# Fused attention and convolution, one core: the order of DVE, ACT and POOL work within a step rearranged

## The chip, the cores and the metric

The kernel runs on one core of a Trainium2 chip. TensorE (PE) multiplies matrices, VectorE (DVE) and ScalarE (ACT) read its results in PSUM, GpSimd (POOL) works on SBUF alone, and SyncE (SP) issues the transfers. The metric is device time in microseconds for one execution. Three runs of the kernel before took 2841.26, 2844.43 and 2851.31 us; the median, 2844.43, is the time to compare with.

## The reference

For each of four batches of 1024 rows by 1024 columns: a modulated RMS norm, attention with 16 heads of 64 and RMS-normalised queries and keys, an output product with a residual, and a causal depthwise convolution with four taps along the rows, whose taps come from `cond`.

```python
scale, shift = jnp.split(emb @ W_emb + b_emb, 2, axis=-1)
xn = _rms_norm(x, g_norm) * (1.0 + scale) + shift
q, k, v = ...                      # xn @ W_qkv, 16 heads of 64
q = _rms_norm(q, g_q)
k = _rms_norm(k, g_k)
attn = jax.nn.softmax(jnp.einsum('bhqd,bhkd->bhqk', q, k) * d ** (-0.5), axis=-1)
o = jnp.einsum('bhqk,bhkd->bhqd', attn, v)
x = x + (o + o @ W_out)            # o with the heads side by side
x = x + conv1d_causal(x, w=cond_2048) + b
```

## The kernel before

Every fp32 operand of a product is split into two fp16 halves, high and low, and a product is three matmuls. The high half is a rounded copy, the low half the difference, made on POOL.

`main` runs 32 **units** u, one for each batch and pair of heads. A unit has eight **steps** p0 to p7, one for each 128 query rows. In step p TensorE makes the scores of both heads (`score`, 12 matmuls of 512 columns); DVE takes each head's row maximum and forms the bias (`maximum`, L1216 and L1219, which also names the start of a step's DVE work); ACT makes the exponentials (`exponent`, L910), and the next step's scores wait for both, since they overwrite the same PSUM. The probabilities are rounded to the high half (`high`: ACT for head 0, L918, DVE for head 1, L1226), POOL makes the low halves (`low`, L1130), and SP transposes each (`transpose_p`). Two steps later `attend` multiplies them with the values in two parts: part 0 ends an odd step, part 1 follows the score of the next. Part 0 waits for the row of inverse sums, which ACT copies behind an odd step's exponentials (`inverse_rows`, L974).

Beside this runs, spread over the steps by hand, other work of other units:
- unit u+1's projections (`project`, p0 to p4) and queries and keys, in two halves: ACT `squares`, DVE `sums`, POOL `half_power` (the power -0.5, L1136), DVE `normalise` (two products, L1242 and L1246), ACT `high_halves` (L941), POOL `half_low` (L1141), TensorE `stacks` (transposes, L811), ACT `read_stacks`. The first score of the next unit needs the stacks that p7 makes;
- in batches 0 to 2, a row block of the next batch (`xs`): DVE `x_mean`, POOL `x_power`, DVE `x_multiply` and `x_shift`, ACT `x_high`, POOL `x_low`;
- from unit 8 on, the output product and convolution of the batch before (`outs`, `fins`): TensorE `out_product` in p5, p6, p7, ACT `read_y`, DVE `convolve` (L1299 to L1314), TensorE `out_transposes`, ACT `read_out`, SP `store_out`. `convolve` treats two chunks of 128 columns by turns: the copy of the halo, the first tap, the ends kept for the next rows, and three multiply-adds for each chunk.

The order on each engine is that of the code in its `unit`; an engine's queue is worked through in order, and semaphores join the engines. Nothing schedules it anew.

## Time and profile before

| | |
|---|---|
| median of three runs | 2844.43 us |
| the profiled execution: time, span | 2844.38 us, 2842.3 us |
| TensorE busy | 2447.5 us (86%) |
| DVE busy | 1947.2 us (69%) |
| POOL busy | 1727.9 us (61%) |
| ACT busy | 1582.1 us (56%) |
| mean granted clock of TensorE | 0.927 |
| main DMA queue, share of 16 engines | 80.1% |

The span runs from the first instruction to the last; the rest of the execution's time lies around it. "Busy" counts an engine's work, also where it is blocked inside an instruction. The first 203.8 us are `prepare` and the first projections, the last 140 the output products of the last batch.

### The profile page before, as it was taken

What the parts mean: (1) busy time and instruction counts of PE and PEld (TensorE: products, weight loads), DVE (VectorE), ACT (ScalarE), POOL (GpSimd) and SP (SyncE); (2) the same over time, 40 slices, a digit from 0 to 9 for tenths busy, and PEclk for the clock granted to TensorE, in tenths of its full rate; (3) what the DMA queues carried; (4) which work ended last, traced back from release to release, by engine and by line L of the source; (5) the groups of instructions that cost most, each with busy time, mean ns of one, the idle gap of its engine ahead of it and who ended that gap; (6) DMA issues with size and microseconds to landing.
All of it is one profiled execution on the core that took longest, in us unless ns stands there. A gap on an engine that the chain in (4) does not pass through costs nothing. (4 is left out here: it accounts for less than half of the span.)

```text
span 2842.3 us, 57564 instructions
## 1 busy us (share of the span) xinstructions
PE 2447.5 (86%) x20690; PEld 1570.7 (55%) x20690; DVE 1947.2 (69%) x2968; ACT 1582.1 (56%) x2575; POOL 1727.9 (61%) x972
## 2 busy tenths in 40 slices
PE   2468788887779999999899999999999998999688
PEld 0034445454446666565566565666566665666477
DVE  7655555555567777787787677778767777777644
ACT  2246565556556666566566666666555565665411
POOL 0057766666766777666667667666666666766510
PEclk8688898888899999999999999999999999999799
DMA  6858777778987897889988888889977878877751
GB/s 252 344 138 167 158 145 154 142 157 167 196 185 163 183 181 162 169 171 200 194 193 174 181 168 177 168 167 220 180 160 153 163 149 161 161 145 146 141 162 60
DMA packets 1234893, 487.28 MB, mean 171 GB/s; under 512 B 1139520, under 2 KB 1196992, under 8 KB 1232064
## 3 DMA queue, kind: packets, MB, share of 16 engines
q1 hardware_dynamic: 1234624, 483.63, 80.1%
q8 instruction: 177, 2.90, 0.4%
q14 instruction: 92, 0.75, 0.1%
HBM read 141.13 MB, written 57.18 MB: 70 GB/s over the span
## 5 line engine op out<-in xcount | busy, mean ns | idle before, releaser
L1130 POOL TENSOR_TENSOR p_pair<-prob,p_pair 128x1024 f16<-128x1024 f32 x512 | 1122.6, 2211 | 618.7 <-ACT p_pair L918 589.3
L799 PE MATMUL proj<-w_sb,xn_sb 128*128 128x384 f16 x6144 | 1029.1, 327 | 34.0 <-DMA xn_sb<-p_pair 29.3
L910 ACT ACTIVATE prob<-scores,bias,l_scale 128x1024 f32<-128x1024 f32 x512 | 616.1, 1203 | 765.7 <-DVE bias L1219 684.4
L1216 DVE TENSOR_REDUCE neg<-scores 128x1 f32<-128x1024 f32 x512 | 623.4, 1218 | 509.3 <-PE scores L748 497.8
L799 PEld LDWEIGHTS proj<-w_sb,xn_sb 128*128 128x128 f16 x6144 | 587.9, 98 | 435.2 <-DMA xn_sb<-p_pair 25.3
L748 PE MATMUL scores<-stack 64*128 64x512 f16 x3072 | 403.2, 398 | 52.7 <-ACT prob L910 34.4
L767 PE MATMUL values<-pT,v_pair 128*64 128x256 f16 x6144 | 431.8, 296 | 11.4 <-ACT inv_row L974 10.1
L767 PEld LDWEIGHTS values<-pT,v_pair 128*64 128x64 f16 x6144 | 345.0, 119 | 110.9 <-issue 82.0
L1226 DVE CAST p_pair<-prob 128x1024 f16<-128x1024 f32 x256 | 217.2, 848 | 157.5 <-ACT prob L910 153.7
L1314 DVE SCALAR_TENSOR_TENSOR acc<-yT,taps,acc 128x256 f32<-128x256 f32 x384 | 272.4, 775 | 5.5
L748 PEld LDWEIGHTS scores<-stack 64*128 64x128 f16 x3072 | 134.5, 98 | 250.2 <-issue 98.1
L823 PE MATMUL proj<-oT_in,wo 128*128 128x256 f16 x2304 | 267.9, 273 | 0.6
L918 ACT ACTIVATE p_pair<-prob 128x1024 f16<-128x1024 f32 x256 | 266.7, 1042 | 0.0
L1136 POOL TENSOR_TENSOR rs<-ms,power 128x16 f32<-128x16 f32 x64 | 202.2, 3159 | 62.7 <-DVE ms L1234 61.5
L823 PEld LDWEIGHTS proj<-oT_in,wo 128*128 128x128 f16 x2304 | 219.6, 98 | 33.7 <-issue 1.8
L811 PE MATMUL misc<-eye,qk_pair 128*128 128x128 f16 x512 | 51.7, 262 | 182.6 <-issue 106.7
L1141 POOL TENSOR_TENSOR qk_pair<-stage,qk_pair 128x512 f16<-128x512 f32 x128 | 157.4, 1252 | 6.5 <-ACT qk_pair L941 6.5
L811 PEld LDWEIGHTS misc<-eye,qk_pair 128*128 128x128 f16 x512 | 40.9, 117 | 190.0 <-issue 189.8
L926 ACT ACTIVATE stage<-proj 128x384 f32<-128x384 f32 x256 | 121.9, 476 | 39.6 <-PE proj L799 39.5
L1306 DVE TENSOR_SCALAR acc<-yT,taps,conv_b 128x256 f32<-128x256 f32 x128 | 128.3, 1043 | 0.0
L1219 DVE TENSOR_SCALAR bias<-neg,l_scale 128x1 f32<-128x1 f32 x512 | 109.7, 214 | 18.1
L1156 POOL TENSOR_TENSOR msx<-msx,power 128x1 f32<-128x1 f32 x32 | 18.0, 564 | 157.5 <-DVE msx L1251 142.9
(127 smaller groups left out, 2303.1 us busy)
## 6 DMA issues: line engine op xcount, KB each, us to landing
w_sb<-w_dram SPq DMA_DIRECT2D x128, 384.0 KB, 3.8
o_dram<-oT_pair SPq DMA_DIRECT2D x128, 128.0 KB, 2.6
out<-acc SPq DMA_DIRECT2D x64, 256.0 KB, 2.6
wq_raw<-in_L_cond_W_qkv SPq DMA_DIRECT2D x8, 1536.0 KB, 10.7
w_dram<-wq_pair SPq DMA_DIRECT2D x8, 1536.0 KB, 7.4
x_in<-in_x SPq DMA_DIRECT2D x24, 512.0 KB, 5.4
oT_in<-o_dram SPq DMA_DIRECT2D x12, 1024.0 KB, 5.9
xr<-in_x SPq DMA_DIRECT2D x24, 512.0 KB, 3.9
```

Of the source, the lines that this page charges most:

```text
L748: last = nc.tensor.matmul(scores[:, h, n * HN:(n + 1) * HN], stack[rows_, par, i, p * P:(p + 1) * P], stack[rows_, par, j, n * HN:(n + 1) ...
L767: last = nc.tensor.matmul(values[DH * h:DH * h + DH, 0:QG].rearrange("p (a n) -> p a n", a=2), v_pair[:, par, 2 * c + h, DH * i:DH * i + D ...
L799: last = nc.tensor.matmul(proj[:, t % 2, 0:6 * DH], xn_sb[:, t, i * K + c, :], w_sb[:, c, j, :], start=(c == 0 and i == j == 0), stop=(c = ...
L823: nc.tensor.matmul(dst, const["wo"][:, c, b, m * P:(m + 1) * P], oT_[:, c, a, :], start=(c == 0 and a == b == 0), stop=False)
L910: nc.scalar.activation(prob[:, h, :], scores[:, h, :], ACT.Exp, bias=bias[:, s:s + 1], scale=const["l_scale"][:, 0:1], accum_out=total[:, ...
L918: nc.scalar.activation(p_pair[:, s % 4, 0, :], prob[:, 0, :], ACT.Copy).then_inc(hi_a, 1)
L1130: nc.gpsimd.tensor_tensor(p_pair[:, s % 4, 1, :], prob[:, h, :], p_pair[:, s % 4, 0, :], ALU.subtract).then_inc(lo_done, 1)
L1136: nc.gpsimd.tensor_tensor(rs[:], ms[:], const["power"][:, 0:4 * KH], ALU.pow).then_inc(h_pw, 1)
L1141: last = nc.gpsimd.tensor_tensor(qk_pair[:, j, 1].rearrange("p t (h d) -> p (t h) d", d=DH), stage[:, hf, :, j * DH:(j + 1) * DH], qk_pair ...
L1216: nc.vector.tensor_reduce(neg[:, s:s + 1], scores[:, h, :], axis=AX.X, op=ALU.max, negate=True).then_inc(max_done, 1)
L1226: nc.vector.tensor_copy(p_pair[:, s % 4, 0, :], prob[:, 1, :]).then_inc(hi_b, 1)
L1314: nc.vector.scalar_tensor_tensor(out=acc[:, m, :], in0=yT[:, m, k:k + QG], scalar=const["taps"][:, k, c:c + 1], in1=acc[:, m, :], op0=ALU. ...
```

## The change

It moves work between places of a unit and splits one helper; no arithmetic is added or left out.
- `high`: DVE rounds head 0 and ACT head 1, in place of the other way round, and DVE does it right behind the maxima.
- `convolve` does one chunk; it is called four times a unit, in p7, p0 and p2 ahead of the maxima and behind `after_lows`, and in p3 behind `high`. Before, it was called in p7 and p1 with two chunks each, behind `high`. `out_transposes` and the store of the second half move from p2 and p4 to p4 and p6, and ACT's `read_out` with them.
- `x_multiply` and `x_shift` both stand in p1 ahead of the maxima, behind `after_lows`; `x_power` stands behind p0's low halves. The row block is loaded in p6 in place of p7.
- Second half of queries and keys: `half_power` stands between the two low halves of p5 (before: ahead of both), `normalise` and ACT's `high_halves` ahead of p6's maxima and exponentials (before: behind them), `half_low` ahead of p6's low halves (before: of p7's), `stacks` ahead of p7's output product (before: behind it).
- `sums` of the first half and `normalise` of the first half stand ahead of the maxima of p3 and p4.
- ACT's `read_projection(w, 1)` stands ahead of p1's exponentials.

```diff
@@ SyncE, unit @@
-                    if p == 4 and fins:
+                    if p == 6 and fins:
                         store_out(T - 1, 1 - par, 1)
...
-                    if p == 6 and more:
-                        load_w(w + 1, 2)
+                    if p == 6:
+                        if xs and not (static(u) and v + 1 >= U):
+                            load_x(v + 1)
+                        if more:
+                            load_w(w + 1, 2)
                     if p == 7:
...
-                        if xs and not (static(u) and v + 1 >= U):
-                            load_x(v + 1)
@@ TensorE, unit @@
                         inverses(u - 1, 3)
+                    if qkv and p == 7:
+                        stacks(w, 1, 1, misc[:], (h_ev, 4 * w + 2))
+                        stacks(w, 1, 0, proj[:, 0, :], (y_ev, 2 * T + 1) if outs else (qkv_ev, K * w + 7))
                     if qkv:
                         for t, q0, q1 in quarters[p]:
...
-                    if qkv and p == 7:
-                        stacks(w, 1, 1, misc[:], (h_ev, 4 * w + 2))
-                        stacks(w, 1, 0, proj[:, 0, :], (y_ev, 2 * T + 1) if outs else (qkv_ev, K * w + 7))
...
-                    if fins and p == 2:
+                    if fins and p == 4:
                         out_transposes(T - 1, 1, (f_ev, 2 * T - 1))
@@ ScalarE @@
             def high(u, p):
-                s = 2 * p
+                s = 2 * p + 1
...
-                nc.scalar.activation(p_pair[:, s % 4, 0, :], prob[:, 0, :], ACT.Copy).then_inc(hi_a, 1)
+                nc.scalar.activation(p_pair[:, s % 4, 0, :], prob[:, 1, :], ACT.Copy).then_inc(hi_b, 1)
...
                             read_stacks(w, 1 - par, 0, 1, 1, proj[:, 1, :])
+                            high_halves(w, 1)
...
-                    if p == 1 and qkv:
-                        read_projection(w, 1)
                     high(u, p)
...
                     if p == 6:
                         read_inverses(u, 1)
-                        if qkv:
-                            high_halves(w, 1)
@@ GpSimd, unit @@
-                    if p == 0 and xs:
-                        x_power(v, par, 2)
...
                             half_low(w, 0)
-                            half_power(w, 1)
+                    if p == 6 and qkv:
+                        half_low(w, 1)
                     if p == 7:
                         o_lower(u, 1)
-                        if qkv:
-                            half_low(w, 1)
                     low(u, p, 0)
+                    if p == 5 and qkv:
+                        half_power(w, 1)
                     low(u, p, 1)
+                    if p == 0 and xs:
+                        x_power(v, par, 2)
@@ VectorE @@
             def high(u, p):
-                s = 2 * p + 1
+                s = 2 * p
...
-                nc.vector.tensor_copy(p_pair[:, s % 4, 0, :], prob[:, 1, :]).then_inc(hi_b, 1)
+                nc.vector.tensor_copy(p_pair[:, s % 4, 0, :], prob[:, 0, :]).then_inc(hi_a, 1)
+
+            def after_lows(u, p):
+                need(dve, lo_done, slot(u, 2 * p))
...
+            def convolve(T, par, hh, i):
+                n = 4 * T + 2 * hh + i
+                m = 2 * hh + i
+                c = 4 * par + m
+                dve.wait_ge(y_ev, 2 * T + hh + 1)
...
+                    if k == TAPS - 1:
...
+                    else:
+                        dve.wait_ge(cv, 4 * n + TAPS - 1 - k)
+                        nc.vector.scalar_tensor_tensor(out=acc[:, m, :], in0=yT[:, m, k:k + QG],
+                                                       scalar=const["taps"][:, k, c:c + 1], in1=acc[:, m, :],
+                                                       op0=ALU.mult, op1=ALU.add).then_inc(cv, 1)
...
                 for p in range(K):
+                    if p == 0 and fins:
+                        after_lows(u, 0)
+                        convolve(T - 1, 1 - par, 0, 1)
+                    if p == 1 and xs:
+                        after_lows(u, 1)
+                        x_multiply(v, par, x_in[:])
+                        x_shift(v, x_in[:])
+                    if p == 2 and fins:
+                        after_lows(u, 2)
+                        convolve(T - 1, 1 - par, 1, 0)
+                    if p == 3 and qkv:
+                        sums(w, 0)
+                    if p == 4 and qkv:
+                        normalise(w, 0)
+                    if p == 6 and qkv:
+                        normalise(w, 1)
+                    if p == 7 and outs:
+                        after_lows(u, 7)
+                        convolve(T, par, 0, 0)
                     maximum(u, p, 0)
                     maximum(u, p, 1)
+                    high(u, p)
...
+                    if p == 3 and fins:
+                        convolve(T - 1, 1 - par, 1, 1)
...
                     if p == 5 and qkv:
                         sums(w, 1)
```

DVE, in the first unit with a convolution, from p6 to p7 (`neg` and `bias` are the maxima, `stage` the queries and keys, `yT`, `acc` and `ends` the convolution). Before:

```order
666 L1242 TENSOR_TENSOR stage<-stage,rs 128x8x128
667 L1246 TENSOR_TENSOR stage<-stage,g_qk 128x8x64
668 L1226 CAST p_pair<-prob 128x1024
669 L1283 TENSOR_TENSOR oT<-values,inv_all 128x256
670 L1216 TENSOR_REDUCE neg<-scores 128x1
671 L1219 TENSOR_SCALAR bias<-neg,l_scale 128x1
672 L1216 TENSOR_REDUCE neg<-scores 128x1
673 L1219 TENSOR_SCALAR bias<-neg,l_scale 128x1
674 L1226 CAST p_pair<-prob 128x1024
675 L1299 TENSOR_SCALAR yT<-ends,carry 128x2x3
676 L1306 TENSOR_SCALAR acc<-yT,taps,conv_b 128x256 x2
```

The same engine and place now, from the cast of p6 on:

```order
748 L1229 CAST p_pair<-prob 128x1024
749 L1275 RECIPROCAL inv<-total 128x4
750 L1278 TENSOR_SCALAR inv_pair<-inv 128x2x2
751 L1280 SCALAR_TENSOR_TENSOR inv_pair<-inv,inv_pair 128x2x2
752 L1289 TENSOR_TENSOR oT<-values,inv_all 128x256
753 L1305 TENSOR_SCALAR yT<-ends,carry 128x3
754 L1309 TENSOR_SCALAR acc<-yT,taps,conv_b 128x256
755 L1312 COPY ends<-yT 128x3
756 L1316 SCALAR_TENSOR_TENSOR acc<-yT,taps,acc 128x256 x3
757 L1219 TENSOR_REDUCE neg<-scores 128x1
758 L1222 TENSOR_SCALAR bias<-neg,l_scale 128x1
```

The convolution stood behind the cast of p7 with two chunks; one chunk now stands ahead of p7's maxima, and the products on `stage` have gone ahead of p6's.

POOL, in a unit of the first batches, from p5 to p7 (`p_pair` are the low halves, `rs` the power, `qk_pair` those of queries and keys, `v_pair` of the values). Before:

```order
184 L1141 TENSOR_TENSOR qk_pair<-stage,qk_pair 128x512 x2
185 L1136 TENSOR_TENSOR rs<-ms,power 128x16
186 L1130 TENSOR_TENSOR p_pair<-prob,p_pair 128x1024 x4
187 L1165 TENSOR_TENSOR oT_pair<-oT,oT_pair 128x256
188 L1141 TENSOR_TENSOR qk_pair<-stage,qk_pair 128x512 x2
189 L1130 TENSOR_TENSOR p_pair<-prob,p_pair 128x1024 x2
190 L1150 TENSOR_TENSOR v_pair<-stage,v_pair 128x8x64
```

The same engine and place now:

```order
214 L1143 TENSOR_TENSOR qk_pair<-stage,qk_pair 128x512 x2
215 L1132 TENSOR_TENSOR p_pair<-prob,p_pair 128x1024
216 L1138 TENSOR_TENSOR rs<-ms,power 128x16
217 L1132 TENSOR_TENSOR p_pair<-prob,p_pair 128x1024
218 L1143 TENSOR_TENSOR qk_pair<-stage,qk_pair 128x512 x2
219 L1132 TENSOR_TENSOR p_pair<-prob,p_pair 128x1024 x2
220 L1167 TENSOR_TENSOR oT_pair<-oT,oT_pair 128x256
221 L1132 TENSOR_TENSOR p_pair<-prob,p_pair 128x1024 x2
222 L1152 TENSOR_TENSOR v_pair<-stage,v_pair 128x8x64
```

The power has moved between the two low halves of p5, and the second pair on `qk_pair` from p7 to the start of p6.

## Rows read from the trace of the kernel before

**Rows 1.** Windows: us, busy by engine (instructions), granted clock, DMA share, GB/s.
```profile
203.80:828.40 624.60, 504.76 (x4116) 299.98 (x4116) 348.06 (x531) 368.18 (x597) 430.02 (x238) 0.88 0.80 158
905.00:2089.10 1184.10, 1107.86 (x9662) 722.86 (x9662) 908.42 (x1320) 722.75 (x1192) 811.13 (x451) 0.97 0.88 180
2089.10:2637.40 548.30, 515.50 (x4512) 336.81 (x4512) 397.62 (x596) 321.88 (x536) 352.82 (x196) 0.97 0.78 153
```

**Rows 2.** Timeline, TensorE, units 21 and 22: start, us, instruction, [idle <-releaser].
```profile
1903.19 1.47 PE L748 MATMUL scores<-stack 64*128 64x512 f16 x12
...
1913.36 1.47 PE L748 MATMUL scores<-stack 64*128 64x512 f16 x12
...
1919.58 1.47 PE L748 MATMUL scores<-stack 64*128 64x512 f16 x12
...
1927.70 1.01 PE L811 MATMUL misc<-eye,qk_pair 128*128 128x128 f16 x8 [3.11 <-issue]
...
1929.49 2.77 PE L767 MATMUL values<-pT,v_pair 128*64 128x256 f16 x24
1932.19 2.06 PE L748 MATMUL scores<-stack 64*128 64x512 f16 x12
...
1943.20 1.47 PE L748 MATMUL scores<-stack 64*128 64x512 f16 x12
...
1950.76 1.50 PE L767 MATMUL values<-pT,v_pair 128*64 128x256 f16 x24
1952.19 1.47 PE L748 MATMUL scores<-stack 64*128 64x512 f16 x12
...
1962.82 1.47 PE L748 MATMUL scores<-stack 64*128 64x512 f16 x12 [0.15 <-ACT prob L910]
```

**Rows 3.** Timeline of DVE, then ACT, then POOL, step p2 of unit 22.
```profile
1958.60 1.21 DVE L1216 TENSOR_REDUCE neg<-scores 128x1 f32<-128x1024 f32 x1
...
1962.80 0.69 DVE L1226 CAST p_pair<-prob 128x1024 f16<-128x1024 f32 x1 [0.63 <-ACT prob L910]
...
1961.47 1.21 ACT L910 ACTIVATE prob<-scores,bias,l_scale 128x1024 f32<-128x1024 f32 x1
...
1964.40 1.06 ACT L934 ACTIVATE x_in<-stage 128x1024 f32<-128x1024 f32 x1
...
1963.79 4.22 POOL L1130 TENSOR_TENSOR p_pair<-prob,p_pair 128x1024 f16<-128x1024 f32 x2 [6.58 <-ACT p_pair L918]
```

**Rows 4.** Timeline of DVE: three places beside POOL's work, one at the end alone.
```profile
1950.50 8.17 DVE L1314 SCALAR_TENSOR_TENSOR acc<-yT,taps,acc 128x256 f32<-128x256 f32 x6
...
1928.07 2.09 DVE L1299 TENSOR_SCALAR yT<-ends,carry 128x6 f32<-128x6 f32 x1
...
639.89 2.58 DVE L1246 TENSOR_TENSOR stage<-stage,g_qk 128x512 f32<-128x512 f32 x1
...
2828.78 2.46 DVE L1314 SCALAR_TENSOR_TENSOR acc<-yT,taps,acc 128x256 f32<-128x256 f32 x6
```

**Rows 5.** Instructions by line: count, busy us, mean ns, idle us before, releaser.
```profile
L1136 POOL TENSOR_TENSOR rs<-ms,power 128x16 f32<-128x16 f32 x64 | 202.2, 3159 | 62.7 <-DVE ms L1234 61.5
L1141 POOL TENSOR_TENSOR qk_pair<-stage,qk_pair 128x512 f16<-128x512 f32 x128 | 157.4, 1252 | 6.5 <-ACT qk_pair L941 6.5
...
L1165 POOL TENSOR_TENSOR oT_pair<-oT,oT_pair 128x256 f16<-128x256 f32 x128 | 88.8, 694 | 22.4 <-ACT oT_pair L987 22.3
L1242 DVE TENSOR_TENSOR stage<-stage,rs 128x1024 f32<-128x1024 f32 x64 | 78.0, 1218 | 6.0 <-POOL rs L1136 6.0
...
L941 ACT ACTIVATE qk_pair<-stage 128x512 f16<-128x512 f32 x128 | 73.4, 625 | 36.6 <-DVE stage L1246 36.5
...
L811 PE MATMUL misc<-eye,qk_pair 128*128 128x128 f16 x512 | 51.7, 262 | 182.6 <-issue 106.7 <-POOL qk_pair L1141 76.0
...
L1257 DVE SCALAR_TENSOR_TENSOR x_in<-x_in,msx,rows 128x1024 f32<-128x1024 f32 x24 | 48.8, 2034 | 0.0
...
L1156 POOL TENSOR_TENSOR msx<-msx,power 128x1 f32<-128x1 f32 x32 | 18.0, 564 | 157.5 <-DVE msx L1251 142.9 <-issue 14.7
```

84 lines of the change are left out of this document (30 added, 54 removed).

## The prediction

> **What bounds the kernel now.** I read the stretches by batch first, then TensorE's timeline over one unit, then what DVE, ACT and POOL do between two scores. A unit is one of 32 passes over eight steps p0 to p7. The windows [rows 1] start at the scores of units 0, 9, 24 and end at those of 8, 24, 31: a unit takes 624.6/8 = 78.1 us in the first batch, 1184.1/15 = 78.9 in units 9 to 23 and 548.3/7 = 78.3 in the last. From unit 8 on PE is busy 94% of the time, at a mean granted clock of 0.97; in the first batch 81% at 0.88. DVE, ACT and POOL are busy 77%, 61% and 69% in units 9 to 23, the DMA engines 88%.
>
> TensorE's steps [rows 2] last 10.2 (p5), 6.2 (p6), 12.6 (p7), 11.0 (p0), 9.0 (p1), 10.6 (p2) us. The one real hole is in p7: 3.11 us of idle before the transposes of the second half of queries and keys (misc L811), and after it the work runs at the lower of the two clock levels: the 24 value matmuls that follow last 2.77 us where others take 1.50, and 12 score matmuls 2.06 where others take 1.47. These transposes waited 182.6 us in all [rows 5]: 24 times some 3 us from unit 8 on, and the rest, some 13 us a unit, in p5 and p7 of the first batch. That is the gain the change can take. In p7 it is 3.1 us of idle, 1.3 of slow value matmuls and 0.9 of slow transposes and scores, which leaves 7.3 of 12.6, and 0.6 at the start of p0.
>
> What decides whether it does is a chain that TensorE's load hides today. I call M the start of a step's first maximum on DVE. From it, in one step [rows 3]: two maxima; the second exponential starts at M+2.9 and the next score starts at M+4.2 (1958.60 to 1962.82, where the gap of 0.15 us says that it was really waited for). ACT's squares end at M+6.9 (1964.40 and 1.06). The inverse row follows the second exponential, so the value matmuls that end an odd step start at M+4.5 at the earliest, and the next score 1.4 later, at M+5.9. So M may lie up to 3.0 us after the score's start in odd steps of 9.0 us and about 5 us in even ones. Usually it lies at 1.5.
>
> **The exchange of the high halves.** DVE now rounds head 0, while ACT is at exponential 1: DVE's cast starts at M+2.85 and takes 0.69 [rows 3], POOL's low halves run from M+3.6, 4.22 us for two, and end at M+7.9. Before they started behind ACT's copy at M+5.2 (1963.79) and ended at M+9.4. That is 1.5 us earlier, and ACT's copy for head 1 (ready at M+5.2) is in time. This alone is a gain, if a small one.
>
> **Convolution in single chunks.** Of four chunks a unit, three (p7, p0, p2) now stand ahead of the maxima and behind a wait for all low halves of the step before; the fourth stands behind p3's cast. Undisturbed, six multiply-adds take 2.46 us [rows 4]; in a single chunk each must wait for the one before, so I count 0.5 for each, 0.6 for halo, first tap and ends: 2.1 us. What is queued behind the wait is the maxima, and for them wait the exponentials, the next score and, in p7, the inverse row for the value matmuls. So M of such a step is no longer where the score ends, but at least the previous M + 7.9 + 2.1 = 10.0. Where such work is not behind POOL's, the two exclude each other: six multiply-adds beside POOL's low halves took 8.17 us, a halo copy of six elements 2.09, a product of two tiles 2.58 in place of 0.69 [rows 4]. One DVE instruction comes through per POOL instruction. The Trainium skill ("SBUF — State Buffer", Who interferes with whom) says the same of instructions with two SBUF inputs, "the other fully blocks"; by it both products of `normalise` block, and that speaks against where the second one now stands (below).
>
> **The links, from M to M**, for units with a row block to fetch and a convolution (9 to 23):
> - p7 to p0: 7.9, then POOL goes straight into low_values (1.2, as long as one of half_low's two instructions [rows 5]), which blocks the first convolution instruction, then 2.0: 11.1.
> - p0 to p1: x_power now stands behind the lows (0.56), o_lower (0.69) gets the port first, then x_multiply (1.1, near the 1.2 of a product of that size alone; its own mean of 2.03 [rows 5] holds blocks) and x_shift (1.2, as `normalise`'s first product, of the same size), both ahead of the maxima: 7.9 + 0.6 + 0.65 + 2.3 = 11.4.
> - p1 to p2: x_low is ready at M+6.9 (x_high is ACT's last work of p1) and starts right behind the lows; it is as long as a low half, 2.1, and blocks the chunk: 12.1.
> - p2 to p3: the sums now stand ahead of p3's maxima: squares at 6.9, sums 1.5: 8.4.
> - p3 to p4: the fourth chunk runs beside both lows and low_values, one instruction per POOL instruction: it ends at about 10.2, then `normalise` 1.9: 12.0.
> - p4 to p6: ACT goes on with copies to M+6.9 (two of 0.63 among them, [rows 5]), reads the last projection, squares (1.06) and o_high to M+8.8; POOL o_lower 9.5, half_low 2.5 to 12.0 with one cast in between, low 0 to 14.2, the power (3.16) to 17.3. Then low 1 starts on POOL at once and `normalise` on DVE beside it. No row of before shows its first product (1.22 [rows 5]) begun under a low half: between 1.2 (not blocked) and 3.2 us (blocked to the end of low 1). I take 3.2, by the row of its second product, 2.58; then 0.65: 21.1.
> - p6 to p7: high_halves 1.25, half_low to M+3.7, the blocked cast to 4.2, two lows to 8.5, chunk 2.1: 10.6.
>
> The sum is 86.7 us a unit against 78.9. With TensorE's work alone it would be 73, today's less the hole.
>
> **What becomes of the hole in p7.** The transposes no longer wait: half_low is done some 3.7 us after M of p6, before score p7 ends. But the value matmuls at the end of p7 need the inverse row, at M7+4.5, and M7 = M6+10.6 is 6.4 us after the score of p7. So p7 lasts 6.4 + 4.5 + 1.4 and some 0.4 for the copy of the stack, 12.7 us: one wait for another, as long. The idle piece is longer than before, so the clock falls as it does now.
>
> **Sum.** Units 9 to 23: 15 x 7.8 = +117. First batch, without convolution: p0 to p4 10.4, 9.0, 10.0, 9.0, 9.0; p5 7.5 (transposes at +4.8 behind half_low); p6 11.4, since M of p6 waits for power and `normalise`; p7 7.8: 74.1, 8 x -4.0 = -32. Last batch, without the row block: p0 11.0, p1 9.0, then M of p3 and p5 fall back to the score, p6 10.1, p7 12.7: 81.5, 7 x 3.2 = +22. Units 8 and 31: +7. The end, one serial chunk pair more: +1. The profiled execution's span of 2842.3 us becomes 2957; it took 2844.4 with what lies around the span, the median of the runs is 2844.4 too. I take off some 10 us for the unit starts at which TensorE waits for nothing that the profile shows: these will fall into slack. Forecast 2950 us. Bounds: with `normalise` unblocked in p6 the sum is 2 x 31 = 62 us lower, 2890; with every link 0.4 longer 2990.
>
> By the skill's rule of exclusion the sum is 2957; if only the halo's and multiply-adds' kinds blocked, it would be 2895. The trace agrees with the rule for the second product and does not show the first.
>
> **Rivals.**
> - *The hole closes and nothing takes its place.* For it: TensorE is 94% busy and the other engines under 80%, so there is room on average. Against it: in p7 M may be 1.1 us after the score at most, and the wait for the lows puts it at 6. Gain 5.8 a unit from 8 on, 4 in the first batch: 2842 - 139 - 32 = 2673. Chance 0.06.
> - *One wait for another in p7, and the rest hidden.* POOL's blocks fall between the chunks, M stays within 3 to 5 us. For it: the lows end 1.5 us earlier, and the 8.17 us beside x_low go. Against: each of p1, p3, p4, p6 has its own reason above to be late. Only the first batch gains: 2842 - 32 = 2810. Chance 0.14.
> - *Half of the links' excess*: unit 80 in the middle, 2842 - 32 + 40, near 2850. Chance 0.06.
> - *The clock gives more away.* With idle pieces of 2 us in p1, p6 and 6 in p7, projections run at the lower level and TensorE is itself late in p0; 1.5 us a unit more: 2990. Chance 0.08. It decides once the steps behind an idle piece are longer than their M chain.
> - *My forecast*, slower than before: 0.66.
>
> Numbers: 2950, its own range 2890 to 2990; the range 2805 to 2990 also takes in the half case and half of the hidden one. A difference of 0.3%, 8.5 us, is about what a measurement can tell. Faster: 0.06 + 0.14 and a bit of the half case, 0.22. Same 0.04. Slower 0.74.
>
> **What would show it.** In the profile after: the wait of misc L811 for POOL or issue all but gone; in its place value matmuls of p7 that wait for ACT's inverse row, 4 to 5 us, 24 times; DVE's convolution waiting for POOL's low half in p7, p0 and p2 with M 4 to 6 us after the score; multiply-adds at 0.48 outside p3; the first product of p6's `normalise` at 3 us; units of 74, 87 and 81 us in the three stretches. I am wrong if units 9 to 23 take under 79 us, if the chunks' wait is short because the lows end before the score does, or if the value matmuls of p7 don't wait.

## The result, and the profile after

The changed kernel takes 3057.98 us (median of four runs, 3057.35 to 3062.61), the kernel before 2844.22 in the same session: ratio 1.0751, with an interval of 1.0729 to 1.0774. It is slower by 7.5%. The direction was forecast; the time, 2950 us, was 108 us too low, and the measured one lies outside the range of 2805 to 2990.

The profiled execution has a span of 3055.5 us. By batch (windows of the changed kernel; the columns are those of [rows 1], and the windows again start at the scores of units 0, 9 and 24):

```profile
202.60:829.80 627.20, 504.30 (x4116) 297.01 (x4116) 483.56 (x531) 373.28 (x598) 429.90 (x238) 0.88 0.80 158
909.90:2244.20 1334.30, 1130.56 (x9660) 730.38 (x9660) 1114.97 (x1379) 732.61 (x1193) 792.72 (x451) 0.96 0.78 159
2244.20:2843.50 599.30, 524.48 (x4510) 341.97 (x4511) 488.64 (x624) 327.38 (x537) 346.04 (x197) 0.96 0.72 140
```

Against [rows 1] the first batch is 2.6 us longer (627.2 and 624.6), units 9 to 23 150.2 (88.95 us a unit and 78.94), the last batch 51.0 (85.6 and 78.3). PE, ACT and POOL are busy for about as long as before in every window. DVE is not: 483.56 and 348.06, 1114.97 and 908.42, 488.64 and 397.62. The clock is the same within 0.01. So DVE's instructions became longer, or were held, and the other engines wait.

Which ones, the groups by line tell (count, busy us, mean ns, idle us before, releaser; they answer to [rows 5]):

```profile
L768 PE MATMUL values<-pT,v_pair 128*64 128x256 f16 x6144 | 411.1, 287 | 81.5 <-ACT inv_row L975 79.5 <-DMA pT<-p_pair 1.3 <-issue 0.5
...
L1278 DVE TENSOR_SCALAR inv_pair<-inv 128x4 f16<-128x4 f32 x128 | 268.3, 2096 | 4.4
L1280 DVE SCALAR_TENSOR_TENSOR inv_pair<-inv,inv_pair 128x4 f16<-128x4 f32 x128 | 261.4, 2042 | 4.4
...
L1248 DVE TENSOR_TENSOR stage<-stage,rs 128x1024 f32<-128x1024 f32 x64 | 137.4, 2148 | 101.7 <-POOL rs L1138 101.2
...
L812 PE MATMUL misc<-eye,qk_pair 128*128 128x128 f16 x512 | 47.9, 249 | 38.7 <-POOL qk_pair L1143 38.7
...
L783 PE MATMUL values<-eye,inv_pair 128*4 128x128 f16 x256 | 36.2, 224 | 204.8 <-DVE oT L1289 203.9 <-DVE inv_pair L1280 0.8
```

The wait that the change was expected to remove is gone: the transposes of queries and keys wait 38.7 us instead of 182.6 [rows 5]. `normalise`'s first product takes 2148 ns on average instead of 1218. And two instructions that the forecast never mentions take 2096 and 2042 ns, 128 times each, together 529.7 us. They are the last two of the three in `invert`, four columns wide. TensorE idles 204.8 us ahead of the `inverses` matmuls (L783), which stand behind them. In the kernel before the same two took

```profile
L1272 DVE TENSOR_SCALAR inv_pair<-inv 128x4 f16<-128x4 f32 x128 | 40.2, 314 | 4.4
...
L782 PE MATMUL values<-eye,inv_pair 128*4 128x128 f16 x256 | 35.5, 221 | 17.8 <-DVE oT L1283 14.1
...
L1274 DVE SCALAR_TENSOR_TENSOR inv_pair<-inv,inv_pair 128x4 f16<-128x4 f32 x128 | 20.8, 163 | 4.4
```

(by line, of before). The timeline of DVE, then of POOL, then of TensorE in the changed kernel shows the mechanism in p2 of one unit (TensorE's score at 2010.98 is already p3's) and, in TensorE's rows, p7 of the same unit from 2054.32 on:

```profile
2002.97 1.81 DVE L1305 TENSOR_SCALAR yT<-ends,carry 128x3 f32<-128x3 f32 x1 [4.59 <-POOL p_pair L1132]
...
2006.75 1.22 DVE L1219 TENSOR_REDUCE neg<-scores 128x1 f32<-128x1024 f32 x1
...
2009.75 0.69 DVE L1229 CAST p_pair<-prob 128x1024 f16<-128x1024 f32 x1 [0.15 <-ACT prob L911]
2010.36 0.17 DVE L1275 RECIPROCAL inv<-total 128x4 f32<-128x4 f32 x1
2010.56 2.11 DVE L1278 TENSOR_SCALAR inv_pair<-inv 128x4 f16<-128x4 f32 x1
2012.70 2.04 DVE L1280 SCALAR_TENSOR_TENSOR inv_pair<-inv,inv_pair 128x4 f16<-128x4 f32 x1
2014.67 0.41 DVE L1289 TENSOR_TENSOR oT<-values,inv_all 128x256 f32<-128x256 f32 x1
```
```profile
2010.52 4.21 POOL L1132 TENSOR_TENSOR p_pair<-prob,p_pair 128x1024 f16<-128x1024 f32 x2 [5.76 <-DVE p_pair L1229]
```
```profile
2010.98 1.47 PE L749 MATMUL scores<-stack 64*128 64x512 f16 x12 [0.16 <-ACT prob L911]
2015.22 0.27 PE L783 MATMUL values<-eye,inv_pair 128*4 128x128 f16 x2 [2.78 <-DVE oT L1289]
...
2054.32 1.47 PE L749 MATMUL scores<-stack 64*128 64x512 f16 x12 [2.16 <-ACT prob L911]
2059.03 0.27 PE L783 MATMUL values<-eye,inv_pair 128*4 128x128 f16 x2 [3.24 <-DVE oT L1289]
2059.25 0.61 PE L812 MATMUL misc<-eye,qk_pair 128*128 128x128 f16 x8
...
2066.18 1.67 PE L768 MATMUL values<-pT,v_pair 128*64 128x256 f16 x24 [2.81 <-ACT inv_row L975]
2067.83 2.75 PE L749 MATMUL scores<-stack 64*128 64x512 f16 x12
```

DVE's cast ends at 2010.44 and lets POOL start its two low halves at 2010.52. DVE's next `inv_pair` instruction starts 0.04 us later and lasts until the first low half is done, the one after it until the second is. `scale_values` follows at 2014.67, ACT and TensorE's inverses follow that. In p7 the transposes start at once behind the inverses, with no wait of their own, and the value matmuls wait 2.81 us for the inverse row: the hole has moved, as forecast, though it is shorter than the 4 to 5 us expected. What stands ahead of it, 3.24 us for the inverses, was not forecast.

From the starts of all scores and first maxima the mean links in units 9 to 23, M to M as in the prediction (us):

| link | forecast | after | inverses ahead of the cast |
|---|---|---|---|
| p0 to p1 | 11.4 | 11.4 | 11.7 |
| p1 to p2 | 12.1 | 11.9 | 11.9 |
| p2 to p3 | 8.4 | 9.8 | 8.8 |
| p3 to p4 | 12.0 | 12.1 | 12.1 |
| p4 to p6 | 21.1 | 21.6 | 21.4 |
| p6 to p7 | 10.6 | 11.3 | 11.3 |
| p7 to p0 | 11.1 | 11.0 | 11.1 |
| unit | 86.7 | 89.0 | 88.2 |

### The profile page after: what moved, and what is told of

Read it like the earlier page. It is cut to its first block, busy times and chain, and to the rows that moved or that the text cites. A ratio compares the mean times of both kernels' runs of the same rounds, so it can differ in the third digit from the quotient of the medians.

```text
span 3055.5 us, 57928 instructions
## 1 busy us (share of the span) xinstructions
PE 2483.6 (81%) x20690; PEld 1583.9 (52%) x20690; DVE 2420.4 (79%) x3096; ACT 1604.0 (52%) x2575; POOL 1702.5 (56%) x972
## 4 chain that ended last, share of the span: by engine, by line
DVE 37%; issue 23%; PE 20%; POOL 11%; ACT 3%; DMA 1%; DVEq 1%; ACTq 0%; SPq 0%; POOLq 0%
PE proj L800 10%; DVE neg L1219 9%; POOL p_pair L1132 7%; DVE inv_pair L1278 6%; DVE acc L1316 4%; DVE stage L1248 4%; PE scores L749 3%; PE values L768 3%; PE proj L824 3%; POOL rs L1138 3%; DVE p_pair L1229 2%; DVE ms L1237 2%; ACT prob L911 2%; DVE ends L1312 2%; DVE bias L1222 2%
## 5 line engine op out<-in xcount | busy, mean ns | idle before, releaser
L1132 POOL TENSOR_TENSOR p_pair<-prob,p_pair 128x1024 f16<-128x1024 f32 x512 | 1094.8, 2157 | 819.5 <-DVE p_pair L1229 818.7
L768 PE MATMUL values<-pT,v_pair 128*64 128x256 f16 x6144 | 411.1, 287 | 81.5 <-ACT inv_row L975 79.5
L824 PE MATMUL proj<-oT_in,wo 128*128 128x256 f16 x2304 | 310.6, 299 | 1.4
L1305 DVE TENSOR_SCALAR yT<-ends,carry 128x3 f32<-128x3 f32 x128 | 69.8, 545 | 259.4 <-POOL p_pair L1132 193.4
L1278 DVE TENSOR_SCALAR inv_pair<-inv 128x4 f16<-128x4 f32 x128 | 268.3, 2096 | 4.4
L824 PEld LDWEIGHTS proj<-oT_in,wo 128*128 128x128 f16 x2304 | 243.1, 108 | 53.4 <-issue 4.3
L1280 DVE SCALAR_TENSOR_TENSOR inv_pair<-inv,inv_pair 128x4 f16<-128x4 f32 x128 | 261.4, 2042 | 4.4
L1316 DVE SCALAR_TENSOR_TENSOR acc<-yT,taps,acc 128x256 f32<-128x256 f32 x384 | 210.6, 549 | 20.1
L1248 DVE TENSOR_TENSOR stage<-stage,rs 128x1024 f32<-128x1024 f32 x64 | 137.4, 2148 | 101.7 <-POOL rs L1138 101.2
L783 PE MATMUL values<-eye,inv_pair 128*4 128x128 f16 x256 | 36.2, 224 | 204.8 <-DVE oT L1289 203.9
L1167 POOL TENSOR_TENSOR oT_pair<-oT,oT_pair 128x256 f16<-128x256 f32 x128 | 104.9, 820 | 143.4 <-ACT oT_pair L988 143.4
## 6 DMA issues: line engine op xcount, KB each, us to landing
wq_raw<-in_L_cond_W_qkv SPq DMA_DIRECT2D x8, 1536.0 KB, 10.2
```

Source lines behind the costliest of these rows:

```text
L768: last = nc.tensor.matmul(values[DH * h:DH * h + DH, 0:QG].rearrange("p (a n) -> p a n", a=2), v_pair[:, par, 2 * c + h, DH * i:DH * i + D ...
L824: nc.tensor.matmul(dst, const["wo"][:, c, b, m * P:(m + 1) * P], oT_[:, c, a, :], start=(c == 0 and a == b == 0), stop=False)
L1132: nc.gpsimd.tensor_tensor(p_pair[:, s % 4, 1, :], prob[:, h, :], p_pair[:, s % 4, 0, :], ALU.subtract).then_inc(lo_done, 1)
L1278: nc.vector.tensor_scalar(inv_pair[:, g % 2, :, 0:2], one_, INV_UP, None, ALU.mult).then_inc(inv_hi, 1)
L1316: nc.vector.scalar_tensor_tensor(out=acc[:, m, :], in0=yT[:, m, k:k + QG], scalar=const["taps"][:, k, c:c + 1], in1=acc[:, m, :], op0=ALU. ...
```

## The experiments

All ratios are to the kernel before in the same session. A unit's time is the distance of its scores' starts in the profiled execution, averaged over units 1 to 7, 9 to 23 and 24 to 30.

| kernel | time | ratio (95%) | units |
|---|---|---|---|
| before | 2844 | 1 | 78.8 / 78.9 / 78.3 |
| after | 3058.0 | 1.0751 (1.0729 to 1.0774) | 78.9 / 89.0 / 85.6 |
| after, inverses ahead of the cast | 3022.0 | 1.0631 (1.061 to 1.0653) | 77.2 / 88.2 / 85.1 |
| and p7's chunk behind the cast | 2944.3 | 1.0357 (1.0335 to 1.0378) | 76.8 / 85.7 / 80.2 |
| and the x work as before | 2913.4 | 1.0242 (1.0226 to 1.0257) | 76.9 / 83.7 / 80.4 |
| and the fourth chunk in p2 | 2882.2 | 1.0129 (1.0112 to 1.0146) | 77.0 / 82.5 / 78.5 |
| after, nothing gated | 2827.5 | 0.9943 (0.9924 to 0.9963) | 76.9 / 79.7 / 77.0 |
| before, gated chunks and x alone | 3041.2 | 1.07 (1.0678 to 1.0723) | 79.0 / 88.7 / 82.9 |
| before, second half early alone | 2864.2 | 1.008 (1.006 to 1.0101) | 78.2 / 79.8 / 79.2 |
| before, exchange alone | 2842.3 | 0.9996 (0.9983 to 1.0009) | 78.9 / 79.1 / 78.5 |
| before, half_low 1 on DVE | 2782.7 | 0.9785 (0.976 to 0.9809) | 76.1 / 77.6 / 75.6 |
| and half_low 0 on DVE | 2784.6 | 0.9788 (0.9766 to 0.9811) | 75.6 / 78.0 / 75.6 |
| half_low 1 on DVE, low values early | 2783.9 | 0.9785 (0.9771 to 0.9798) | 76.1 / 77.2 / 76.8 |
| and the second convolution in p2 | 2819.1 | 0.991 (0.9897 to 0.9924) | 76.1 / 79.0 / 77.7 |

### The inverses ahead of the cast

```
+ if p == 0 and begun: invert(u - 1, 3, 1 - par)
+ if p in (2, 4, 6): invert(u, p // 2 - 1, par)
  high(u, p)
  ...
- invert(...)   # at both places behind high
```

> The changed kernel, with the three small instructions of invert ahead of DVE's cast again (they were ahead of it in the kernel before, behind it in the changed one). Theory (the links from M to M as forecast, and what the forecast missed is that two of invert's instructions are blocked by one low half each, 2 us apiece, 128 times): with them out of the low halves' way the forecast's own sum holds, 2955 us (2935 to 2975), units of 74, 87 and 81.5 us in the first batch, in units 9 to 23 and in the last. Rival (invert's 4 us lie where DVE would idle anyway, and it is the gated chunks that cost more than forecast): 3035 to 3058, units within 0.5 us of the changed kernel's 78.9, 89.0, 85.6.

Measured: 3021.96 us, 36 less than after. It lies between the two answers. The inverses are again short (L1278 308 ns on average, and TensorE's idle before L783 falls from 204.8 to 19.7 us), but most of what TensorE no longer waits for there it waits for later, since the gated maxima come no earlier: its idle time before the value matmuls grows from 81.5 to 179.0 us. This shows the missed step, and that it explains a third of the 108 us. Of the 36 us, 15 lie in the first batch, 11 in units 9 to 23, 4 in the last batch, and 9 behind the start of unit 31 (212.0 us from there to the end, 203.0 with the inverses ahead); elsewhere 2 are lost. Part of the rest stands in this kernel's timeline of a step p7 (TensorE, then DVE):

```profile
2130.36 2.77 PE L768 MATMUL values<-pT,v_pair 128*64 128x256 f16 x24 [4.19 <-ACT inv_row L975]
2133.06 2.74 PE L749 MATMUL scores<-stack 64*128 64x512 f16 x12
```
```profile
2117.58 0.67 DVE L1278 TENSOR_SCALAR inv_pair<-inv 128x4 f16<-128x4 f32 x1
...
2123.38 0.62 DVE L1305 TENSOR_SCALAR yT<-ends,carry 128x3 f32<-128x3 f32 x1 [2.77 <-POOL p_pair L1132]
...
2125.87 1.22 DVE L1219 TENSOR_REDUCE neg<-scores 128x1 f32<-128x1024 f32 x1
```

M7 is 2125.87, the value matmuls start at M7+4.5, as forecast. But behind 4.19 us of idle they run at the lower clock level (granted clock 0.50 from 2130.40 to 2133.00) and take 2.77 us, so the next score comes at M7+7.2 and not at M7+5.9. The forecast said that the clock falls there and still counted the 1.4 us of the higher level. On average the 24 value matmuls at the end of p7 take 2.73, 2.65 and 2.77 us in the three stretches of this kernel. In the changed kernel itself they do so in the first batch alone (2.77 us); from unit 9 on they take 1.51 us.

### The second half alone

```
+ normalise(w, 1) ahead of p6's maxima (was behind them)
+ high_halves(w, 1), half_low(w, 1) in p6 (were in p7)
+ stacks(w, 1, ...) first in p7
```

> The kernel before, with the second half of queries and keys alone moved as in the change (normalise, high_halves and half_low in p6 ahead of maxima, exponentials and low halves, transposes ahead of p7's product), the power staying ahead of both low halves of p5. Theory: the transposes' wait goes, and since no chunk gates the maxima of p7, nothing takes its place: p6 a little longer (7.1 for 6.2, normalise blocked by a low half), p7 7.5 to 8 in place of 12.6; 24 x -3.8 and 8 x -6: 2705 us (2690 to 2745). Rival (the hole in p7 turns into another wait, whatever gates the maxima): 2820 to 2850.

Measured: 2864.21 us, slower by 0.8% instead of faster by 5%: a clear miss. Steps p7 fall from 13.0 to 9.7 us, but p6 grows from 6.2 to 8.9 and p1 from 9.4 to 11.0. DVE, then POOL, around p6:

```profile
1998.88 3.14 DVE L1241 TENSOR_TENSOR stage<-stage,rs 128x1024 f32<-128x1024 f32 x1 [2.80 <-POOL rs L1135]
2002.06 2.50 DVE L1245 TENSOR_TENSOR stage<-stage,g_qk 128x512 f32<-128x512 f32 x1
2004.48 1.21 DVE L1215 TENSOR_REDUCE neg<-scores 128x1 f32<-128x1024 f32 x1
```
```profile
1995.51 3.34 POOL L1135 TENSOR_TENSOR rs<-ms,power 128x16 f32<-128x16 f32 x1 [0.38 <-DVE ms L1233]
1998.81 5.19 POOL L1129 TENSOR_TENSOR p_pair<-prob,p_pair 128x1024 f16<-128x1024 f32 x2
```

The power is the release of both: POOL goes straight on with its low halves, and DVE's products start 0.07 us after them. Both are blocked, 5.6 us where [rows 5] have 1.22 and 0.69 was expected for the second, and the maxima of p6 stand behind them. Here is also the row that the prediction did not have: a first product of `normalise` begun under a low half takes 3.14 us. Its upper bound was the right one.

### The exchange alone

```
- ACT:  s = 2 * p     ... p_pair <- prob[:, 0], hi_a
- DVE:  s = 2 * p + 1 ... p_pair <- prob[:, 1], hi_b
+ ACT:  s = 2 * p + 1 ... p_pair <- prob[:, 1], hi_b
+ DVE:  s = 2 * p     ... p_pair <- prob[:, 0], hi_a
```

> The kernel before, with the exchange of the high halves alone (DVE head 0, ACT head 1; invert stays ahead of the cast). Theory: low halves end 1.5 us earlier in each step, which shortens the hole in p7 by as much and the first batch's waits too: 2790 us (2765 to 2815). Rival (DVE's work behind the cast, x_multiply and the convolution, meets both low halves from their start and loses what is gained): 2840 to 2870.

Measured: 2842.27 us, ratio 0.9996: nothing, and the interval excludes the expected 1.9%. In p6, the step whose low halves set the hole in p7, they do not end earlier: on average 10.1 us behind M in units 9 to 23, 9.9 before. The cast that now releases them stands behind the second half's `normalise` there (DVE and POOL of this kernel, then POOL of before at the same place; the scores of p7 start at 2004.14 and 1997.57):

```profile
2003.93 0.69 DVE L1246 TENSOR_TENSOR stage<-stage,g_qk 128x512 f32<-128x512 f32 x1
2004.54 0.69 DVE L1226 CAST p_pair<-prob 128x1024 f16<-128x1024 f32 x1
```
```profile
2005.30 4.22 POOL L1130 TENSOR_TENSOR p_pair<-prob,p_pair 128x1024 f16<-128x1024 f32 x2 [4.08 <-DVE p_pair L1226]
```
```profile
1998.06 4.68 POOL L1130 TENSOR_TENSOR p_pair<-prob,p_pair 128x1024 f16<-128x1024 f32 x2 [3.53 <-ACT p_pair L918]
```

Only in p0, p1 and p2 do the low halves end earlier, by 1.8, 1.3 and 0.9 us. Where DVE's convolution or x work is behind the cast, it is blocked by the same two low halves either way (the links p7 to p0 and p1 to p2 are 15.1 and 13.6 us, 15.2 and 13.9 before).

### The gated work alone

```
+ after_lows(u, p); convolve(.., one chunk)     ahead of the maxima in p7, p0, p2
+ after_lows(u, 1); x_multiply; x_shift         ahead of the maxima in p1
```

> The kernel before, with the convolution in single chunks and x_multiply and x_shift ahead of the maxima, behind the wait for the low halves, as in the change; high halves and the second half of queries and keys as before. Theory (a gated step's M is the last M plus the low halves' end, here 9.4, plus the gated work): p7 15 us, p1 14, p2 12 in units 9 to 23, 87 us a unit; 2980 us (2950 to 3010). Rival (single chunks behind the low halves cost little by themselves, and the loss comes from the other two parts): 2840 to 2880.

The output transposes, their copy and store, `x_power` and `read_projection(w, 1)` stand where the change has them too. Measured: 3041.18 us. The theory's mechanism, larger than expected: units 9 to 23 take 88.7 us for 87, with p7 at 17.4 us for 15, p1 at 14.1 for 14 and p2 at 11.3 for 12. Two waits of this kernel (us in all, times, longest):

```profile
DVE yT L1304 <- POOL p_pair L1132: 326.0, 70, 5.2
...
PE values L767 <- ACT inv_row L974: 186.1, 48, 6.9
```

This part alone costs 196 us; all of the change costs 214. The parts nearly add up: 196, the 36 of the inverses behind the cast, less some 17 by which the rest of the change is faster than before (the last kernel of the next section), are some 215.

### Taking the gates away one by one

First p7's chunk goes behind p7's cast, without its wait:

```
- if p == 7 and outs: after_lows(u, 7); convolve(T, par, 0, 0)   # ahead of the maxima
+ if p == 7 and outs: convolve(T, par, 0, 0)                      # behind high
```

> The changed kernel with the three inverse instructions ahead of the cast (3022 us), and in addition the one convolution chunk of p7 moved behind p7's cast, without its wait for the low halves of p6; the chunks of p0 and p2 and the x work stay ahead of the maxima behind their waits. Theory (the wait itself makes the unit long: nothing of p7's maxima can start before POOL has ended p6's low halves): the link p6 to p7, 11.3 us in units 9 to 23, falls to 6 or so; of that the link p7 to p0 gives back about 1, since the chunk now runs beside p7's low halves, and what is left is limited by TensorE's own step of p6 (9.5 us). Net some 3 to 4.4 us in 23 units: 3022 - 100 = 2920 us (2900 to 2955). Rival (the single chunks cost their own time and their blocks wherever they stand): the chunk takes three blocks of 2.1 us beside POOL behind the cast, and the time stays at 3010 to 3040.

Measured: 2944.29 us, 78 less. The link p6 to p7 falls from 11.3 to 6.6 us, p7 to p0 rises from 11.1 to 13.3. The theory holds; the net is 2.6 us in units 9 to 23 and 4.9 in the last batch, where 3 to 4.4 were expected for all, and the time is inside the range, 24 us above its middle value.

Then the x work goes back to where it was:

```
- if p == 1 and xs: after_lows(u, 1); x_multiply; x_shift   # ahead of the maxima
+ x_power first on POOL in p0, x_multiply behind p0's cast, x_shift behind p1's maxima
```

> The changed kernel with the inverses ahead of the cast and p7's chunk behind p7's cast (2944 us), and in addition the x work where it was before: its power first on POOL in p0, its product behind the cast of p0, its sum behind the maxima of p1. The chunks of p0 and p2 stay gated ahead of the maxima, the fourth stays behind the cast of p3. Against the kernel without any gated work (2827.5 us) the one with the x work and two chunks gated takes 6.0 us a unit more in units 9 to 23 and 3.2 more in units 24 to 30, which have no x work. Theory (the gates add up, each is paid in its own step): the x gate is the difference, 2.8 us in each of 16 units with both: 2944 - 45 = 2900 us (2885 to 2915). Rival (one gate makes the others free, since M is late already): 2930 to 2950, or all of it comes back only when the last gate goes.

Measured: 2913.44 us, 31 less where 45 were expected; all of it in units 9 to 23 (2.0 us each), nothing in the last batch, which has no x work. The price adds up, if not fully: x_multiply now runs beside the low halves and takes 2.58 us on average, 1.61 behind the gate in the kernel without this edit, so some of the gate's price comes back as a block.

Then the fourth chunk goes from p3's cast to p2's gate:

```
- if p == 3 and fins: convolve(T - 1, 1 - par, 1, 1)        # behind high
+ if p == 2 and fins: ... convolve(.., 1, 0); convolve(.., 1, 1)
```

> The changed kernel with the inverses ahead of the cast, p7's chunk behind its cast and the x work as before (2913 us), and in addition the fourth chunk moved from behind p3's cast, where it is blocked by two low halves and low_values, to p2, gated ahead of the maxima together with the third. 86 us still lie between 2913 and the kernel without gated work (2827.5). Theory (what is left is the fourth chunk alone: in units 24 to 30 the links p3 to p4 to p5 to p6 take 12.1 + 6.0 + 15.4 = 33.5 us against 31.0 without it, and the gates in p0 and p2 meet an M that the x work and the inverse row make late anyway): the links from p3 on come back to 8.8 + 9 + 13.2, the second gated chunk adds 2 us to the link p1 to p2, which is slack in units 24 to 30 (M 2.9 us behind the score) and costs some in units 9 to 23: 2.8 x 7 + 1 to 2 x 16 less: 2875 us (2855 to 2895). Rival (the gates in p0 and p2 are what costs): two chunks in one gate make it worse, 2915 to 2950.

Measured: 2882.19 us, 31 less, as the theory had it (2875). In the last batch the links p3 to p6 come to 7.7 + 9.4 + 12.8 = 29.9 us from 33.5, and the second gated chunk leaves the step p2 at 10.0 us, since M of p2 is then 5.1 us behind its score, what an even step bears. In units 9 to 23 it does cost: M of p2 is 8.9 us behind its score, the step p2 grows from 11.0 to 13.1 us, and the unit gains 1.2 us where the last batch gains 1.9. A gate costs where the step has no slack; behind p3's cast the chunk costs three blocks.

Last, nothing gated:

```
  convolution in pairs of chunks behind the casts of p1 and p7, x work as before
  kept from the change: exchange, sums and normalise ahead of the maxima,
  power between p5's low halves, half_low(w, 1) in p6, stacks first in p7
```

> The changed kernel with the inverse instructions ahead of the cast and without the gated part: the convolution in two-chunk pieces behind the casts of p1 and p7, the x work and the output transposes where they were before; kept are the exchanged high halves, the sums and the normalise work ahead of the maxima, the power between the two low halves of p5, and the second half's low halves in p6. Theory (of the whole loss, the gated work carries some 200 us and the inverses behind the cast 36; the second half's early normalising is about neutral): the time comes to 2790 to 2860, near before's 2844, I take 2830. Rival (normalising ahead of the maxima costs as much as the gates do, since M of p6 waits there for POOL's power and is blocked by the low half behind it): 2880 or more.

Measured: 2827.50 us, faster than before by 0.6%, 2830 was forecast. So the rest of the change is a small gain, and the way from after to here is 36 (inverses), 78 (p7's gate), 31 (x gate), 31 (fourth chunk) and 55 us (the gates of p0 and p2 together with the single chunks and the place of the output transposes, which these runs don't part).

### The hole at its cause

In the kernel before the hole of p7 ends when POOL has done `half_low(w, 1)`, which stands behind p6's two low halves and o_lower. DVE is idle at that time. So that work alone was moved, in the kernel before:

```
  POOL p7:  o_lower(u, 1)
-           half_low(w, 1)
  DVE p7:   maxima
+           half_low(w, 1)    # the same two subtractions, nc.vector
            high(u, 7)
```

> The kernel before with one edit: the two subtractions that give the second half's low halves of queries and keys (128x512 each, 2.5 us on POOL in p7, behind o_lower) are done by DVE in p7, between the maxima and the cast. In unit 22 of before DVE is free at 2001.9, the high halves are there since 1999.3, POOL ends its low halves at 2002.7, o_lower 0.7 later and this work only at 2006.0, when TensorE's transposes start. Theory (the hole of 3.1 us in p7 is POOL's queue and nothing else): DVE's first subtraction is blocked until 2002.7, the second runs beside o_lower or behind it, the transposes start at 2004.0 instead of 2006.1, the value matmuls behind them need an inverse row that is there at 2004.4: 2.1 us a unit, and 0.5 to 1 more where the clock no longer falls: 31 x 2.1 = 65, up to 90: 2775 us (2750 to 2800). Rival (one wait for another: the subtractions delay the cast and the next step's work as much as they bring): 2825 to 2860.

Measured: 2782.72 us, ratio 0.9785. DVE, POOL and TensorE of this kernel in a step p7 (its score starts at 1955.96, the next one at 1965.26):

```profile
1960.23 2.51 DVE L1250 TENSOR_TENSOR qk_pair<-stage,qk_pair 128x512 f16<-128x512 f32 x2
1962.66 0.68 DVE L1224 CAST p_pair<-prob 128x1024 f16<-128x1024 f32 x1
...
1966.19 5.18 DVE L1322 SCALAR_TENSOR_TENSOR acc<-yT,taps,acc 128x256 f32<-128x256 f32 x6
1971.29 1.21 DVE L1214 TENSOR_REDUCE neg<-scores 128x1 f32<-128x1024 f32 x1
```
```profile
1956.45 4.67 POOL L1130 TENSOR_TENSOR p_pair<-prob,p_pair 128x1024 f16<-128x1024 f32 x2 [3.53 <-ACT p_pair L918]
1961.08 1.12 POOL L1165 TENSOR_TENSOR oT_pair<-oT,oT_pair 128x256 f16<-128x256 f32 x1
```
```profile
1962.84 0.61 PE L811 MATMUL misc<-eye,qk_pair 128*128 128x128 f16 x8 [1.87 <-issue]
...
1963.83 1.50 PE L767 MATMUL values<-pT,v_pair 128*64 128x256 f16 x24
1965.26 1.47 PE L748 MATMUL scores<-stack 64*128 64x512 f16 x12
```

The two subtractions are blocked too, one by the low half, one by o_lower: 2.51 us in all. They still end 1.6 us after POOL's last low half of p6 (1962.74 and 1961.12); on POOL, behind o_lower, they ended 3.3 us after it. The idle piece shrinks from 3.11 to 1.87 us, and behind the shorter one the value matmuls take 1.50 us instead of 2.77 and the scores 1.47 instead of 2.06 [rows 2]. Steps p7 fall from 13.0 to 10.2 us on average; in this unit 1.2 us is the idle time and 1.7 the clock (1.3 in the value matmuls, 0.4 in the transposes). The granted clock is 0.50 over the value matmuls before (1929.5 to 1932.2) and 1.00 here (1963.8 to 1966.7). In units 9 to 23 the value matmuls at the end of p7 take 1.63 us on average, 2.46 before, and p1 gives 1.6 back (9.4 to 11.0): TensorE is through with p7 earlier, but the convolution behind p7's cast is not, and M of p0 is now 5.9 us behind its score.

The same for the first half, and the low values at another place:

```
  DVE p5:  + half_low(w, 0)  ahead of sums(w, 1)          (POOL p5: - half_low(w, 0))
```

> As the kernel with the second half's low halves on DVE, and the first half's too: in p5 DVE does them between the maxima and the sums of the second half, instead of POOL (2.3 us there, ahead of the power). Theory: in units 9 to 23 nothing waits for them in p5; the sums and with them POOL's power come 1.4 us later, so that p5's low halves end 1.4 us later (1995.9 in unit 22 instead of 1994.5), which p6's second exponential just feels; in the first batch the transposes of p5 start 1 us earlier. 0 to -10 us against the other kernel, 2770. Rival: the later power delays the normalise work of p6 and so brings the hole back in part: +20 to +40 us against the other kernel, 2795 to 2815.

```
  POOL p7: - low_values(w, 1)      POOL p6: + low_values(w, 1)  ahead of the low halves
```

> The kernel with the second half's low halves on DVE (2783 us), and the second half's low values (128x512, 1.2 to 1.3 us on POOL) ahead of p6's low halves instead of behind p7's. In its trace POOL idles from 1970 or so in that place of the unit before, some 3.5 us between p5's and p6's low halves, and ACT has the high values 6 us earlier. Behind p7's low halves it blocks the third of the convolution's multiply-adds: 1968.41 and 1.37 us instead of 0.47, and the next maximum, at 1971.29, is 5.9 us behind its score. Theory (p0 and p1 are set by DVE's M there): 0.9 us in each of the 22 units with a convolution: 2783 - 20 = 2763 us (2755 to 2772). Rival (TensorE sets p0 to p2 anyway, or the normalise work of p6 is blocked by it in turn): 2780 to 2795.

Measured: 2784.59 and 2783.91 us, both no different from 2782.72. The first gains 0.5 us a unit in the first batch and loses 0.4 in units 9 to 23. The second gains 0.4 us in units 9 to 23, half of what was expected, and loses 1.2 in the last batch, where the order of two starts decides (DVE, then POOL, in a step p6 there; then both at the same place of the kernel without this edit):

```profile
2258.23 0.30 DVE L1280 TENSOR_SCALAR inv_pair<-inv 128x4 f16<-128x4 f32 x1
...
2260.50 2.64 DVE L1224 CAST p_pair<-prob 128x1024 f16<-128x1024 f32 x1
```
```profile
2257.34 1.15 POOL L1150 TENSOR_TENSOR v_pair<-stage,v_pair 128x512 f16<-128x512 f32 x1
2260.46 2.12 POOL L1130 TENSOR_TENSOR p_pair<-prob,p_pair 128x1024 f16<-128x1024 f32 x1 [1.97 <-ACT p_pair L918]
```
```profile
2262.09 0.69 DVE L1224 CAST p_pair<-prob 128x1024 f16<-128x1024 f32 x1
```
```profile
2262.18 4.67 POOL L1130 TENSOR_TENSOR p_pair<-prob,p_pair 128x1024 f16<-128x1024 f32 x2 [3.04 <-ACT p_pair L918]
```

The low values hold an inverse instruction for 0.13 us more than its 0.17. So DVE's cast starts 0.04 us after the low half and not 0.09 before it, and takes 2.64 us instead of 0.69; p7's maxima stand behind it, 3.5 us behind the score on average instead of 1.5. All seven casts of p6 in units 24 to 30 take 2.6 us, and none in units 9 to 23. That is the rival's block, one instruction further on.

```
  DVE:  - convolve(T - 1, 1 - par, 1) behind p1's cast     + behind p2's cast
  its output transposes in p4, their copy at p4's end, the store in p6
```

> As the kernel with the low values ahead of p6's low halves, and the second half of the convolution behind the cast of p2 instead of p1 (its output transposes in p4, their copy at the end of p4, the store in p6). Behind p1's cast it is blocked three times, by two low halves and x_low (2.45, 2.34 and 2.35 us for multiply-adds of 0.47), and the link p1 to p2 is 13.9 us, p2 to p3 5.8. Theory (behind p2's cast it meets two low halves only, and p3 to p5 have 3 us of slack in front of their maxima): p1 falls from 11.0 to 9.5 us in units 9 to 23, the links p1 to p2 and p2 to p3 come to 9 and 10 to 11: 1.5 x 16 = 24 us less than the other, 2738 (2725 to 2755). Rival (the lateness is only moved: p3 to p5 run late instead, and a late inverse row makes the value matmuls of p3 and p5 wait): within 10 us of the other or slower.

Measured: 2819.12 us, 35 us slower than without this edit: the rival. (The expected 2738 starts from the 2763 expected of the kernel without it, not from its measured 2784.) The links come out as expected (8.9 and 12.9 us where 13.9 and 5.8 were), but M of p3 is then 4.4 us behind its score, more than the 3 us an odd step bears, and p3 grows from 9.4 to 10.6 us, while p1 falls by 0.2 only. p4 and p5 grow by 0.4 and 1.0 us too; that the transposes or their copy do this wasn't tested.

## Why the prediction was wrong

**The step that was left out.** The prediction goes through exchange, chunks, sums, `normalise`, power and half_low, but says nothing of `invert`, which the change moves from ahead of DVE's cast to behind it. Together with the exchange, which makes that very cast the release of POOL's low halves, it puts two four-column instructions under two low halves in each even step. "One DVE instruction comes through per POOL instruction" was in the text, with the halo copy of six elements at 2.09 us beside it [rows 4]; it was applied to what was wide. Undone alone: 36 us. The list of moves ahead of the prediction leaves this one out too.

**The terms that were mis-sized.** With the inverses back, 62 us remain between the sum of 2957 and a span of 3019.2. By stretch:
- The first batch, 612.5 us for 592.8. Its p7 was forecast at 7.8 us and takes 10.3: 1.3 are the value matmuls at the lower clock level, M7+4.5 to M7+7.2 and not 5.9, and 1.3 that M7 is 2.8 us behind its score and not 1.5.
- Units 9 to 23, 88.2 us for 86.7, 23 us. There M sets the unit and the slow matmuls lie beside it. The link p6 to p7 is 0.7 longer: the low halves end at M+8.7 and not at M+8.5, since half_low holds an inverse instruction ahead of the cast (0.67 us for 0.17), and p7's chunk loses another 0.4 behind them, in 5 of the 15 units because o_lower holds its halo copy (0.62 us for 0.22), in the others because it starts at M+9.2. p2 to p3 is 0.4 longer, since the sums start at M+7.0 to M+7.3 and not at M+6.9. The others are 0.4 together.
- The last batch, 85.1 for 81.5, 25 us: p7 takes 15.0 for 12.7, 1.3 of it the clock again and 0.7 that M7 is 7.1 us behind its score, not 6.4; most of the rest, 1.4 us, lies in p2 to p5, where p5 takes 11.7 us, 10.5 with the fourth chunk in p2.

Outside these stretches the kernel is 6 us shorter than summed. So the clock's term was 1.3 us in 15 units, some 20 us, in the kernel with the inverses ahead. In the changed kernel the value matmuls are slow in the 8 units of the first batch only, some 10 us; why not in the others stays open. The last 10 us of the 108 are those that the forecast took off its own sum for unit starts; no run shows them.

**What was right.** Six of the seven links are within 0.4 us in the kernel with the inverses ahead. The gates as the chief cost: 196 us alone. The transposes' wait gone and the inverse row's in its place. The block of `normalise`'s first product, taken at its upper bound: 3.1 us; the forecast chose between 1.2 and 3.2 by a row of another product, so this bound was a choice that came true. The range was too narrow at the top because it covered errors in the sizes of the links, and neither a step left out nor the slower work behind a hole that the text itself forecast.

**The exchange** was called "a gain, if a small one". Alone it is none. In the changed kernel the low halves do end at M+7.8 to M+8.0, as forecast, in units 9 to 23 in all steps but p5 (M+11.7) and p6 (M+8.4); in p6 that rests on `normalise` standing ahead of the maxima, which brings its own wait. The first batch was to gain 32 us by all moves together; with the inverses ahead it gained 12.

**The rivals.** "The hole closes and nothing takes its place" could be had, in part: not by doing the second half earlier, but by giving its last subtractions to the engine that is idle in p7. Its gain of 5.8 us a unit was counted too high: the slow scores stand in it twice, in the 0.9 and in the 0.6. "The clock gives more away", chance 0.08, is the rival that had the mis-sized term, at 1.5 us a unit in p0 where 1.3 in p7 were measured.

## What to carry to other kernels

When an edit changes which instruction releases an engine whose instructions exclude one's own, as POOL's do DVE's here, list every instruction that stands behind that release on the releasing engine, however small: here four columns were held as long as 1024, and the order of two starts 0.04 us apart decided. Before moving a whole chain to close a hole, look at the one instruction that ends the hole and at who is idle just then; moving those two subtractions brought 2.2%, moving the chain ahead of them to an earlier place cost 0.8%. And where a forecast says that the clock will fall at a place, price the work behind that place at the lower level as well as at the higher one.
